# A perceiver layer in one program block: the branch flag by semaphore, LayerNorm statistics in the first loop, FFN weights transposed behind it

## The reference

```python
x = x + xattn(layernorm(x), ctx, ctx, w_q, w_k, w_v, w_o)   # 16 heads of 64, causal mask of -10000
x = x + attn(layernorm(x), Wq, Wk, Wv, Wo, bo)              # 16 heads of 16, causal
x = x + ffn(layernorm(x), w_gate, w_up, w_down)             # 256 -> 704 -> 256

def fp4_linear(x, w):        # blocks of 16 along the last axis
    return einsum('bsk,nk->bsn', fp4_quant_dequant(x), fp4_quant_dequant(w))
def ffn(x, w_gate, w_up, w_down):
    h = silu(fp4_linear(x, w_gate)) * fp4_linear(x, w_up)
    return fp4_linear(h, w_down)
```

## Time and profile before

| | us |
|---|---|
| median of 3 runs | 589.01 (588.13 to 589.04) |
| profiled execution, its own time | 590.92 |
| its span, first to last instruction | 589.5 |
| PE busy | 539.6 (92%) |
| DVE busy | 445.9 (76%) |
| ACT busy | 233.5 (40%) |
| POOL busy | 45.4 (8%) |

### The profile page before, as it was taken

How to read it: one execution, slowest core, us unless ns; L and a number is a source line. 1 busy time by engine, 2 the same in 40 slices (tenths; PEclk the granted TensorE clock), 3 DMA queues, 4 the chain that set the end, 5 groups by cost and what they waited for, 6 DMA issues and landing times. The chain is left out here.

```text
span 589.5 us, 18962 instructions
## 1 busy us (share of the span) xinstructions
PE 539.6 (92%) x7942; PEld 428.0 (73%) x7942; DVE 445.9 (76%) x876; ACT 233.5 (40%) x477; POOL 45.4 (8%) x83
## 2 busy tenths in 40 slices
PE   4979999999999999999835889999999999999865
PEld 3768888888888888988623666777777777777643
DVE  3637789777887977787817479988888888888842
ACT  1323233323323332332304656555555555554211
POOL 5000100000000000000003011111111111111100
PEclk9979999999999999999966999999999999999977
DMA  8992221022122102221200000000000000000000
GB/s 254 343 272 73 71 71 44 27 71 71 71 71 71 35 37 71 71 71 73 74 4 2 2 2 2 9 9 9 9 9 9 9 9 9 9 9 11 9 9 19
DMA packets 13800, 31.01 MB, mean 53 GB/s; under 512 B 976, under 2 KB 10704, under 8 KB 11728
## 3 DMA queue, kind: packets, MB, share of 16 engines
q1 hardware_dynamic: 13776, 30.67, 15.8%
HBM read 28.57 MB, written 2.10 MB: 52 GB/s over the span
## 5 line engine op out<-in xcount | busy, mean ns | idle before, releaser
L328 PEld LDWEIGHTS bank<-x_xcT,xwk 128*128 128x128 f32 x512 | 61.3, 197 | 2.8 <-issue 1.1
L328 PE MATMUL bank<-x_xcT,xwk 128*128 128x128 f32 x512 | 61.7, 280 | 1.4 <-ACT x_xcT L426 1.4
L350 PE MATMUL bank<-xwv,x_xcT 128*128 128x512 f32 x128 | 61.1, 621 | 1.0
L319 PE MATMUL bank<-x_xcT,xwq 128*128 128x128 f32 x512 | 59.8, 275 | 0.0
L375 PE MATMUL bank<-xwo,x_oT 128*128 128x256 f32 x256 | 58.0, 380 | 0.9 <-ACT x_oT L443 0.9
L319 PEld LDWEIGHTS bank<-x_xcT,xwq 128*128 128x128 f32 x512 | 58.5, 192 | 0.0
L457 ACT COPY x_k_blocks<-bank 64x512 f32<-64x512 f32 x32 | 18.6, 581 | 87.2 <-PE bank L328 87.1
L375 PEld LDWEIGHTS bank<-xwo,x_oT 128*128 128x128 f32 x256 | 47.5, 190 | 7.2 <-issue 1.5
L1118 PE MATMUL bank<-wdT,f_hqT 128*128 128x256 f32 x192 | 48.3, 404 | 4.3 <-DVEq L1403 2.3
L1273 ACT ACTIVATE a_kblocks<-bank,head_rows 128x256 f32<-128x256 f32 x128 | 48.4, 499 | 0.0
L1142 PE MATMUL bank<-wgT,f_xqT 128*128 128x192 f32 (+1 forms) x128 | 43.0, 481 | 3.6 <-DVE f_out L1344 3.6
(11 more groups left out here) (150 smaller groups left out, 931.7 us busy)
## 6 DMA issues: line engine op xcount, KB each, us to landing
x_ctx_slab<-in_ctx_dram SPq DMA_DIRECT2D x16, 1028.0 KB, 4.8
out_dram<-f_out SPq DMA_DIRECT2D x16, 128.0 KB, 1.7
xall<-in_x_dram SPq DMA_DIRECT2D x1, 1280.0 KB, 16.6
x_first_keys<-in_ctx_dram SPq DMA_DIRECT2D x4, 320.0 KB, 12.6
xwk<-in_L_xattn_w_k_dram SPq DMA_DIRECT2D x1, 1024.0 KB, 5.0
xwq<-in_L_xattn_w_q_dram SPq DMA_DIRECT2D x1, 1024.0 KB, 7.1
xwv<-in_L_xattn_w_v_dram SPq DMA_DIRECT2D x1, 1024.0 KB, 10.3
xwo<-in_L_xattn_w_o_dram SPq DMA_DIRECT2D x1, 1024.0 KB, 12.8
```

The costliest lines, as they stand in the source:

```text
L319: last = nc.tensor.matmul(bank67[:, j // 4, (j % 4) * P:(j % 4 + 1) * P], xwq[:, k, j * P:(j + 1) * P], xcT[:, k, :], start=(k == 0), stop ...
L328: last = nc.tensor.matmul(bank[2 + j // 4][:, (j % 4) * P:(j % 4 + 1) * P], xwk[:, k, j * P:(j + 1) * P], xcT[:, KD + k, :], start=(k == 0 ...
L350: last = nc.tensor.matmul(bank45[:, half, :], xcT[:, KD + k, :], xwv[:, k, half * 512:(half + 1) * 512], start=(k == 0), stop=(k == KD - 1))
```

## The change

The three blocks become three Python functions that return one program for each engine, and one block runs them one behind another, so that no barrier stands between. The branch waits on a semaphore raised behind the flag. The LayerNorm statistics for self-attention are taken in the first loop (`take_stats`), and the power for 15 tiles is taken ahead of the all-reduce, that of the last tile behind it. All 13 weight slices (now 352 columns) lie in the first loop, and the 12 groups of FFN transposes stand behind PE's and ACT's work of the first stage, over five PSUM banks. The memsets of `a_v` and `f_hqT` move to the start. The all-keys branch retakes the statistics if it runs. Everything else is moved by indentation only.

```diff
-        WB = -(-NBLK // (T - W0))
+        NS = T - 1 - W0
+        WB = -(-NBLK // NS)
+        wt_bank = (bank[2], bank[3], bank45[:, 0, :], bank45[:, 1, :], bank67[:, 1, :])
+        N_PARTS = ((0, T - 1), (T - 1, T), (0, T))
+        def statistics(part, step):
+            t0, t1 = N_PARTS[part]
+            for t in range(t0, t1):
+                last = nc.vector.bn_aggr(n_mv[:, t, :], n_stats[:, t, :])
+            step(last)
+            nc.vector.tensor_scalar(n_ve[:, t0:t1], n_mv[:, t0:t1, 1], LN_EPS, None, ALU.add).then_inc(s_n_ve, 1)
+        def roots(pool, part):
+            t0, t1 = N_PARTS[part]
+            pool.wait_ge(s_n_ve, part + 1)
+            nc.gpsimd.tensor_tensor(n_rstd[:, t0:t1], n_ve[:, t0:t1], neg_half[:, t0:t1], ALU.pow)\
+                .then_inc(s_n_rstd, 1)
+        def shifts(dve, part):
+            t0, t1 = N_PARTS[part]
+            dve.wait_ge(s_n_rstd, part + 1)
+            nc.vector.scalar_tensor_tensor(out=n_shift[:, t0:t1], in0=n_mv[:, t0:t1, 0], scalar=-1.0,
+                                           in1=n_rstd[:, t0:t1], op0=ALU.mult, op1=ALU.mult)\
+                .then_inc(s_n_shift, 1)
...
-                        nc.gpsimd.memset(wdT[:, FC - 1, :], 0.0)
+                        nc.gpsimd.memset(wdT[:, FC - 1, :], 0.0).then_inc(s_clear, 1)
+                        nc.gpsimd.memset(a_v[:], 1.0).then_inc(s_clear, 1)
+                        nc.gpsimd.memset(f_hqT[:], 0.0).then_inc(s_clear, 1)
...
+                    roots(pool, 0)
                     pool.wait_ge(s_tops, 1)
                     step(nc.gpsimd.partition_all_reduce(tops_all[:], tops[:], P, bass.bass_isa.ReduceOp.max))
                     step.end()
                     pool.sem_inc(s_topsall, 1)
+                    roots(pool, 1)
...
+                    pe.wait_ge(s_wq, NS)
+                    for n, (parts, rows, width, dst) in enumerate(groups):
+                        if n >= len(wt_bank):
+                            pe.wait_ge(s_wtc, n + 1 - len(wt_bank))
+                        for src, m, r, col in parts:
+                            last = nc.tensor.transpose(wt_bank[n % len(wt_bank)][0:m, col:col + r],
+                                                       w_raw[0:r, src:src + m], ident[0:r, 0:r])
+                        last.then_inc(s_wt, 1)
+                    pe.wait_ge(s_wtc, len(groups))
...
+                    act.wait_ge(s_clear, 3)
+                    for n, (parts, rows, width, dst) in enumerate(groups):
+                        act.wait_ge(s_wt, n + 1)
+                        nc.scalar.copy(dst, wt_bank[n % len(wt_bank)][0:rows, 0:width]).then_inc(s_wtc, 1)
...
+                    def take_stats(t):
+                        dve.wait_ge(s_x1, t + 2)
+                        nc.vector.bn_stats(n_stats[:, bass.ds(t, 1), :].rearrange("p o e -> p (o e)"), tile_of(xall, t))\
+                            .then_inc(s_n_st, 1)
...
                             normalise(t + 2)
+                        if residual:
+                            take_stats(t - 1)
                         if spread:
                             spread_k(t + 1)
...
                     watch_context(T - 1)
+                    take_stats(T - 2)
+                    n_step = Chain(dve, s_n, 2)
+                    n_step.begin(0)
+                    dve.wait_ge(s_n_st, T - 1)
+                    statistics(0, n_step)
                     add_residual(T - 1)
                     dve.wait_ge(s_hb, 1)
                     fin(nc.vector.tensor_reduce(tops[0:XP, 1:2], bank[0][0:XP, 0:2], AX_X, ALU.max))
                     dve.sem_inc(s_tops, 1)
+                    take_stats(T - 1)
+                    dve.wait_ge(s_n_st, T)
+                    statistics(1, n_step)
...
+                    dve.sem_inc(s_known, 1)
+                    shifts(dve, 0)
+                    shifts(dve, 1)
...
             def failed(eng):
+                eng.wait_ge(s_known, 1)
                 return eng.If(eng.value_load(needs_all_keys[0:1, 0:1], min_val=0, max_val=1))
...
+                    pool.wait_ge(s_load, 16 * 5)
+                    pe.wait_ge(s_load, 16 * 5)
```

More of the change, by code:

```diff
@@ new lines, in perceiver_layer @@
+        for c0 in range(0, FC, 2):
+            for rows, cs in ((P, [c for c in (c0, c0 + 1) if F - c * P >= P]),
+                             (FR, [c for c in (c0, c0 + 1) if F - c * P < P])):
+                if cs:
+                    groups.append(([(w_down_at + k * F + c * P, rows, P, (i * KD + k) * P)
+                                    for i, c in enumerate(cs) for k in range(KD)], rows, len(cs) * D,
+                                   wdT[0:rows, cs[0]:cs[-1] + 1, :].rearrange("p c d -> p (c d)")))
@@ L143, in weight_slice @@
             w_step.end()
[L145 to L202, removed]
@@ new lines, in dve_program @@
+                        for t in range(T):
+                            last = nc.vector.bn_stats(n_stats[:, t, :], xall[:, t, :])
+                        last.then_inc(s_n_st, 1)
+                        dve.wait_ge(s_n_st, T + 1)
+                        n_step = Chain(dve, s_n, 1)
+                        n_step.begin(2)
+                        statistics(2, n_step)
+                        shifts(dve, 2)
+                return sp_program, pool_program, pe_program, act_program, dve_program
@@ L1215, in step, with act_program @@
                             turn_o(t)
+                    pe.wait_ge(s_load, 16 * 5)
                     steps(pe, step)
-                @block.scalar
-                def _(act):
-                    def copy_weights(first):
-                        for n, (parts, rows, width, dst) in list(enumerate(groups))[first:first + per_step]:
-                            act.wait_ge(s_wt, n + 1)
-                            nc.scalar.copy(dst, wt_bank[n % len(wt_bank)][0:rows, 0:width]).then_inc(s_wtc, 1)
+                def act_program(act):
                     def turned(src, n):
@@ L1293, in step @@
                             tanh(t - 2)
-                        if project and not gate:
-                            copy_weights((t + 1) * per_step)
                         if project:
@@ L1435, in step, with _ @@
                             add_out(t - 3)
-                    n_step = Chain(dve, s_n, 3 * len(N_PARTS))
-                    n_step.begin(0)
-                    for t0, t1 in N_PARTS:
-                        for t in range(t0, t1):
-                            last = nc.vector.bn_stats(n_stats[:, t, :], xall[:, t, :])
-                        n_step(last)
-                        for t in range(t0, t1):
-                            last = nc.vector.bn_aggr(n_mv[:, t, :], n_stats[:, t, :])
-                        n_step(last)
-                        n_step(nc.vector.tensor_scalar(n_ve[:, t0:t1], n_mv[:, t0:t1, 1], LN_EPS, None, ALU.add))
-                        dve.sem_inc(s_n_ve, 1)
-                        if t0 == 0:
-                            shifts(0)
-                    n_step.end()
-                    weight_slice(Chain(dve, s_dw, 9), T - 1 - W0)
-                    shifts(1)
-                    steps(dve, step)
+                    steps(dve, step)
+                return sp_program, pool_program, pe_program, act_program, dve_program
+        stages = cross_attention(), all_keys(), rest()
+        with nc.Block() as block:
+            @block.sync
+            def _(sp):
+                for sp_program, _, _, _, _ in stages:
+                    sp_program(sp)
+            @block.gpsimd
+            def _(pool):
+                for _, pool_program, _, _, _ in stages:
+                    pool_program(pool)
+            @block.tensor
+            def _(pe):
+                for _, _, pe_program, _, _ in stages:
+                    pe_program(pe)
+            @block.scalar
+            def _(act):
+                for _, _, _, act_program, _ in stages:
+                    act_program(act)
+            @block.vector
+            def _(dve):
+                for _, _, _, _, dve_program in stages:
+                    dve_program(dve)
 def block_scales(nc, step, w, amax, scale, inv):
```

405 lines of the change are left out of this document (205 added, 200 removed).

## The result

| | before | changed |
|---|---|---|
| median, us | 590.35 (15 runs, 587.68 to 593.08) | 586.98 (15 runs, 585.30 to 588.76) |
| ratio, 95% interval | | 0.9943 [0.9927, 0.9959] |
| profiled execution's span, us | 589.5 | 586.8 |
| tile 0's turn on PE, us | 314.84 | 311.79 |
| first gate product on PE, us | 345.84 | 344.60 |

The change makes the kernel 0.57% faster, 3.4 us at this median; forecast were 4.2 us (0.71%), in a range from 1.4 to 9.0.

What follows compares the result with a forecast made beforehand. PE's idle hole between the stages, from barriers, jump and POOL's code switch, was taken as the bound. Gains of 1.5 + 1.65 + 1.05 = 4.2 us turn 589.0 into 584.8 us, range 580.0 to 587.6.

Steps and rivals of the forecast that it cites:

- The hole and its causes: PE nearly idle between the stages, 15.4 us from flag to first tile: barriers and jump, and POOL's code switch.
- First loop on DVE at no cost: Each step's extra bn_stats (0.46 us) and wider weight slice (0.35) fit in DVE's waits of 1.86 and 0.36 us.
- The variance of 15 tiles ready ahead of the residual addition, its power on the path: End of first stage: variance ready at about 297.4 in DVE's idle time; POOL's power, 2.82 us, runs 297.5 to 300.3.
- The switch toward the all-reduce at 6.8 us: POOL's code change behind the 15-tile power takes 6.8 us, so all-reduce starts at 307.1 and flag stands at 308.0.
- PE's jump as before: Behind the flag, PE needs 5.1 us from release to jump's end; tile 0 turned at 313.3, gain 1.5 us.
- Steps -1 to 1, 2.7 us more: Second pipeline's fill: without weight transposes and copies, step 0 gains 1.65 us and step 1 gains 1.05 us.
- The switch back, covered: POOL's return for the last tile's power ends at 314.9, DVE's shift at 315.1; covered by over 6 us.
- The signs: Changed profile: all-reduce at about 307, 36 weight transposes 298 to 304, tile 1's copy 3 us earlier, tile 2's scores 4.
- Rival B: POOL's switch ahead of the all-reduce costs nothing; gain 8.6 us, kernel 580.4 us; chance 0.15.
- rival C: POOL's switch toward the all-reduce is dearer than the one back; at 13.6 us the kernel takes 591.6; chance 0.07.
- D: Taking weights out of the fill gives nothing, other ACT work holds steps 0 and 1; 587.5 us; chance 0.07.

Runs made afterwards that it cites:

- changed_again: The changed kernel itself, nothing altered, measured again beside three other kernels; ratio to the kernel before 0.9959.
- weights_in_fill: The changed kernel with the 12 groups of weight transposes and copies put back into steps -1, 0 and 1; ratio to the kernel before 1.0005.
- the filler: The changed kernel with 8 and 10 unused identity transposes on PE in steps -1 and 1, where PE stood idle; ratio to the kernel before 0.9906.

## Why the prediction was right

The forecast was 4.2 us less and 3.4 were measured (2.4 by changed_again's ratio), but terms of the sum were off in opposite directions, and that the total came out near is in part luck: in the profile of the changed kernel tile 0 gained twice the 1.5 us of the sum, and the fill, which was to give 2.7 us, took 1.8.

*The hole and its causes*: right. *First loop on DVE at no cost*: right; all of the cover behind the slice is used. *The variance of 15 tiles ready ahead of the residual addition, its power on the path*: right, 297.92 to 300.66 for 297.5 to 300.3.

*The switch toward the all-reduce at 6.8 us*: right in kind, 5.7 in size (300.66 to 306.37), and 5.6 to 6.1 in four other profiles. The error is in taking the one row there was, the switch back, for both; the switch back cost 6.8 before and 6.7 to 7.4 in six later profiles. The Trainium skill's about 6 us (GPSIMD Engine Reference, section 2.1) is nearer to the first of the two than my row was.

*PE's jump as before*: 3.3 us in place of 4.05, so tile 0 is turned at 311.79 and not at 313.3. Together these two made the gain up to tile 0 3.05 us instead of 1.5, with 0.36 us lost in the first stage on the way.

*Steps -1 to 1, 2.7 us more*: this is the step that failed. The prediction said that PE is at half clock up to tile 0's scores in both kernels, and "from then on each step repeats as now". It costed the removal of the weights as if PE kept its clock, but with them PE lost the work that filled its waits. Half-clock stretches put 0.8 to 4.6 us back (fills of 29.1 to 32.9 us where 28.3 was the sum). The one near tile 2's scores costs 0.9 to 1.6 us (3.25 to 3.99 us up to the gate product, against 2.36); by seven profiles against four it comes with the removal. The one near tile 0's scores costs some 2.5 us (9.89 against 7.35) and stands also in weights_in_fill, so the removal is not shown to be its cause. The two terms themselves were mis-sized as well: 1.82 us in place of 1.65 in step 0, 0.52 in place of 1.05 in step 1, together 2.3 and not 2.7. That PE at rest falls to half its clock is what the Trainium skill says too (TensorE: Matmul & The Clock Gate, Part 1). Here PE was not at rest when it fell: in the stretches ahead it worked 1.20 of 3.50 and 0.73 of 3.40 us.

*The switch back, covered*: right; the power of the last tile at 314.0 and the shift at 314.62, while ACT came to tile 1 at 320.12.

*The signs*: the all-reduce, its pair and the weight transposes stand where they were forecast. Tile 1's copy came 4.1 us earlier (322.38 for 326.45; forecast 3), tile 2's scores 2.9 us (340.61 for 343.48; forecast 4).

Rival B (a free switch) and rival C (dearer than 11 us) are excluded by the 5.7; D by the filler.

## What to carry to other kernels

Before an operation is moved onto GpSimd between two others, look for MODIFY_POOL_CONFIG in its sequencer's rows: a pair that lay in a long wait comes due on the path as soon as another kind of instruction stands ahead of it. Replacing the one instruction that needed the other code, two small matmuls and a reduction in its place, won twice as much as the whole restructuring (1.1 to 1.2% against 0.4 to 0.6%). And when work is taken off PE in a stretch where PE waits anyway, read the granted clock of that stretch afterwards; the work may have been what kept it up.

## What the runs showed of the hardware that was not expected

The two directions of POOL's switch differ: 5.6 to 6.1 us toward the all-reduce (five profiles), 6.7 to 7.4 back to the power (seven). PE's jump over the all-keys code took between 3.3 and 4.05 us in otherwise like kernels, ACT's 0.05 us; what sets it within that was not tried. The first stage is the same code up to the flag but for small parts, yet spread_k of the step at 208.66 stood anywhere from 206.98 to 209.96 in the profiles. The traces show most of the cause: behind a wait of PE at about 35 to 38 us, while the first loads run, its clock is at half for 3.4 us in six profiles (spread_k at 206.98 to 208.22) and for 6.8 us in eight (208.66 to 209.96). That alone moves the time by some 1.5 us, with no line of the change behind it, and is one reason why ratios of one kernel differed by 0.3% between measurements. What decides between 3.4 and 6.8 was not tried.
